# A two-layer decoder on one core: a shared first convolution, identity products for TensorE, an earlier signal of the residual sum, and first keys laid down later

## The reference, cut to what matters

```
layer 0: softmax attention, 16 heads of 16 features; queries and keys through a
         3-tap convolution; per token tau, delta = sigmoid(w2 . gelu(depthwise
         3-tap convolution of x)); scores * tau + delta; then output projection
         cross attention to the context (softmax over features)
         8 experts, each token to its best 2, 640 slots each, relu
layer 1: causal linear attention with rotary angles
         context-query attention (c2q, q2c), linear over 4 parts
         16 experts, each takes 64 tokens of an entry (after Sinkhorn), gelu
```

## Time and profile before

| | |
|---|---|
| median of 3 runs | 2402.48 us (2394.66 to 2403.40) |
| profiled execution, its own time | 2401.25 us |
| its span in the trace | 2399.5 us |
| PE busy | 2083.1 us, 87% |
| DVE, ACT, POOL busy | 1568.1, 1270.4, 1097.1 us |
| mean granted PE clock | 0.937 of full |

### The profile page before, as it was taken

The page is one execution under the profiler, slowest core; times in us unless marked ns, Lnnn a source line. Parts: engine busy times, 40 slices in busy tenths (PEclk is TensorE's granted clock), DMA queues, the critical chain, the costliest instruction groups (busy, mean ns, idle before and its releaser), DMA issues. The chain is left out here.

```text
span 2399.5 us, 47249 instructions
## 1 busy us (share of the span) xinstructions
PE 2083.1 (87%) x17382; PEld 1468.1 (61%) x17382; DVE 1568.1 (65%) x3061; ACT 1270.4 (53%) x2058; POOL 1097.1 (46%) x1252
## 2 busy tenths in 40 slices
PE   7599999995887299967999969961999999999998
PEld 5466666663665177755666648841667667676675
DVE  5378888885897655547888746667555555555553
ACT  2266666664343166635666635532664664654653
POOL 2988888861221122226655314301545445455443
PEclk9799999997998599989999969985999999999999
DMA  5000000000002233311111000041434434434332
GB/s 226 1 2 1 0 0 0 0 1 6 8 9 71 77 130 114 114 44 32 32 30 26 0 11 18 15 141 69 114 75 110 105 80 109 101 101 100 87 78 30
DMA packets 66919, 136.00 MB, mean 57 GB/s; under 512 B 11201, under 2 KB 52369, under 8 KB 59921
## 3 DMA queue, kind: packets, MB, share of 16 engines
q1 hardware_dynamic: 37264, 87.65, 10.5%
q0 software_dynamic: 29568, 47.21, 10.0%
HBM read 100.22 MB, written 34.60 MB: 56 GB/s over the span
## 5 line engine op out<-in xcount | busy, mean ns | idle before, releaser
L3375 ACT ACTIVATE f_h<-bank,f_b 128x512 f32<-128x512 f32 x256 | 176.1, 688 | 275.6 <-PE bank L176 268.9
L3418 DVE TENSOR_TENSOR f_hidlo<-f_h,f_hidhi 128x512 f16<-128x512 f32 x256 | 177.1, 692 | 165.7 <-ACT f_hidhi L3376 161.9
L176 PE MATMUL ring<-f_w2hi,f_hidhi 128*128 128x256 f16 x1024 | 279.2, 273 | 5.9 <-DVE f_hidlo L3418 3.6
L176 PE MATMUL ring<-f_w2lo,f_hidhi 128*128 128x256 f16 x1024 | 279.1, 273 | 0.0
L176 PE MATMUL ring<-f_w2hi,f_hidlo 128*128 128x256 f16 x1024 | 279.1, 273 | 0.0
L3475 POOL DMA_INDIRECT out<-f_y,f_to_row x128 | 203.4, 1589 | 96.6 <-DVE f_y L3433 50.7
L176 PE MATMUL bank<-f_xthi,f_w1hi 128*128 128x512 f16 x512 | 194.6, 380 | 0.0
L176 PE MATMUL bank<-f_xtlo,f_w1hi 128*128 128x512 f16 x512 | 194.6, 380 | 0.0
L176 PE MATMUL bank<-f_xthi,f_w1lo 128*128 128x512 f16 x512 | 194.5, 380 | 0.0
L3376 ACT ACTIVATE f_hidhi<-bank,f_b 128x512 f16<-128x512 f32 x256 | 174.3, 681 | 0.0
L3460 POOL DMA_INDIRECT f_xg<-tokens,f_from_row x128 | 149.2, 1166 | 47.9 <-issue 34.6
(11 more groups left out here) (621 smaller groups left out, 6012.8 us busy)
## 6 DMA issues: line engine op xcount, KB each, us to landing
f_raw<-in_e_w SPq DMA_DIRECT2D x32, 1024.0 KB
c_raw<-in_e_w SPq DMA_DIRECT2D x16, 1024.0 KB, 5.1
slots_out<-c_y SPq DMA_DIRECT2D x40, 128.0 KB, 4.1
x<-in_x SPq DMA_DIRECT2D x1, 4096.0 KB
tokens<-c_xn SPq DMA_DIRECT2D x16, 256.0 KB, 2.7
tokens<-f_xn SPq DMA_DIRECT2D x16, 256.0 KB, 2.5
out<-x SPq DMA_DIRECT2D x1, 4096.0 KB, 14.3
wb<-in_wb SPq DMA_DIRECT2D x1, 3096.0 KB, 33.0
```

What stands on the lines that cost most here:

```text
L176: mm = pe.matmul(out, left[a], right[b], start=first and n == 0, stop=last and n == 2)
L3375: act.activation(h32[n % 4][:, :], src, ACT.Gelu_apprx_tanh, bias=bias).then_inc(sig["h_full"], 1)
L3418: dve.tensor_tensor(hid_v[1][:, it, at], h32[n % 4][:, :], hid_v[0][:, it, at], ALU.subtract).then_inc(sig["h_lo"], 1)
```

## The change

It has four parts.

1. In the `front` of the first attention GpSimd makes only part 0 of the convolution of twins[0]; VectorE makes parts 1 to 3 (`convolve_first`): for each of the two groups of a part one scaled copy and two multiply-adds of 128x256, with a wait on its own counter after each tap. They stand behind both `low_x` and ahead of `take_q`. ACT's first `gelu` waits for the three parts too. GpSimd's order becomes: part 0 of twins[0], part 0 of twins[1], `high_keys` of twins[0], parts 1 to 3 of twins[1]. The turns after that are as before.
2. `keep_busy(pe, mem, bank, n)` issues n products of the fp16 identity with itself, 128 by 512 columns, into a bank that is free then. They stand at nine places: 16 in the front of the first attention; 8 and 16 in that of the cross attention; 28 at the start of the 8 experts; 22 and 32 in the front of the linear attention, the 22 behind a new wait for w_low_made; 12 ahead of the context attention and 6 in each of its first pair's six `products`; 18 and 12 in the first `turn_rows` of the 16 experts. That is 200 in all.
3. `residual_add` raises x_updated with the sum, waits for x_updated itself, and then makes the statistics. Its unused branch with a bias goes.
4. The later `high_keys` of part 1 (first keys laid down later).

```diff
+def keep_busy(pe, mem, bank, n):
+    for _ in range(n):
+        pe.matmul(bank.rearrange("p (r c) -> p r c", c=P), mem.ident16[:, :],
+                  mem.ident16[:, :].unsqueeze(1).to_broadcast([P, 4, P]), start=True, stop=True)
...
-def residual_add(dve, sig, mem, b, now, ready, update, bias, order, tmp):
+def residual_add(dve, mem, b, now, ready, update, updated):
     dve.wait_ge(ready, now)
     xb = mem.x[:, bass.ds(b * W2, W2)]
...
-        order.step(dve.tensor_tensor(xb, xb, update, ALU.add))
-    order.wait()
+    dve.tensor_tensor(xb, xb, update, ALU.add).then_inc(updated, 1)
+    dve.wait_ge(updated, now)
     for t in range(NT):
-        ins = dve.bn_stats(mem.stats[...], mem.x[...])
-    return ins
+        dve.bn_stats(mem.stats[...], mem.x[...])
...
 first attention, PE front
                     sum_tau_delta(w, j)
+                    keep_busy(pe, mem, twins[1].ring_bank[1], 16)
 ACT front
+                    act.wait_ge(sig["first_convolved"], 3)
                     gelu(w, j)
 POOL
-                    if part == 3:
+                    if part == (0 if first else 3):
                         pool.sem_inc(u["conv_done"], 1)
                 def front(w, j, v):
-                    for u in twins:
-                        for part in range(4):
-                            convolve(u, j, part)
-                        if u.p == 0:
+                    convolve(w, j, 0, first=True)
+                    for part in range(4):
+                        convolve(twins[1], j, part)
+                        if part == 0:
                             high_keys(w, j)
 DVE
+                def convolve_first(u, i, part):
+                    groups = (2 * part, 2 * part + 1)
+                    dve.wait_ge(u["x_pad_ready"], i.now)
+                    for k in range(TAPS):
+                        for c in groups:
+                            w = mem.cols[:, dwc + TAPS * c + k:dwc + TAPS * c + k + 1]
+                            x, out = u.xp[:, (c // 2) % 2, k:k + S], u.dw_v[:, c, :]
+                            if k == 0:
+                                ins = dve.tensor_scalar(out, x, w, mem.cols[...], ALU.mult, ALU.add)
+                            else:
+                                ins = dve.scalar_tensor_tensor(out=out, in0=x, scalar=w, in1=out, ...)
+                        order.step(ins)
+                        order.wait()
+                    dve.sem_inc(sig["first_convolved"], 1)
                 def front(w, j, v):
                     for u in twins:
                         low_x(u, j)
+                    for part in range(1, 4):
+                        convolve_first(w, j, part)
                     take_q(w, j)
 cross attention, PE front
+                    keep_busy(pe, mem, w.bank[2], 8)
                     turn_x(w, j)
+                    keep_busy(pe, mem, w.bank[2], 16)
 8 experts, PE
+                keep_busy(pe, mem, bank[5], 28)
                 turn_slots(Turn(0, 1), True)
 linear attention, PE front
+                    pe.wait_ge(sig["w_low_made"], 1)
+                    keep_busy(pe, mem, twins[1].high, 22)
                     turn_x(w, j)
...
                     project_v(w, j)
+                    keep_busy(pe, mem, twins[1].high, 32)
                     turn_queries(w, j, 0)
 context attention, PE
+                        if ago is None:
+                            keep_busy(pe, mem, twins[0].out, 6)
+                        else:
...
                 pe.wait_ge(sig["w_q_ready"], 1)
+                keep_busy(pe, mem, twins[0].out, 12)
 16 experts, PE, turn_rows
+                        if first and k == 2:
+                            keep_busy(pe, mem, bank[5], 12)
...
+                keep_busy(pe, mem, bank[5], 18)
                 turn_rows(Turn(0, 1), True)
```

More of the change, by code:

```diff
@@ L517, in transpose_entry @@
     return ins
-def residual_add(dve, sig, mem, b, now, ready, update, bias, order, tmp):
+def residual_add(dve, mem, b, now, ready, update, updated):
     dve.wait_ge(ready, now)
     xb = mem.x[:, bass.ds(b * W2, W2)]
-    if bias is not None:
-        order.step(dve.tensor_tensor(tmp, xb, update, ALU.add))
-        order.wait()
[L527 to L530, removed]
-        order.step(dve.tensor_tensor(xb, xb, update, ALU.add))
-    order.wait()
+    dve.tensor_tensor(xb, xb, update, ALU.add).then_inc(updated, 1)
+    dve.wait_ge(updated, now)
     for t in range(NT):
-        ins = dve.bn_stats(mem.stats[:, bass.ds((b * NT + t) * 6, 6)], mem.x[:, bass.ds(b * W2 + t * D, D)])
-    return ins
+        dve.bn_stats(mem.stats[:, bass.ds((b * NT + t) * 6, 6)], mem.x[:, bass.ds(b * W2 + t * D, D)])
 def transpose_stack(pe, mem, out, stack, t):
@@ L978, in _, with convolve @@
                 order = Order(pool, sig["pool_step"])
-                def convolve(u, i, part):
+                def convolve(u, i, part, first=False):
                     if part == 0:
@@ L1130, in update @@
                 def update(u, i):
-                    residual_add(dve, sig, mem, i.before * 2 + u.p, i.now, u["out_made"], u.high, None, order, None
-                                 ).then_inc(u["x_updated"], 1)
+                    residual_add(dve, mem, i.before * 2 + u.p, i.now, u["out_made"], u.high, u["x_updated"])
+                def convolve_first(u, i, part):
[6 more added lines that the diff above has]
+                            if k == 0:
+                                ins = dve.tensor_scalar(out, x, w, mem.cols[:, dwb + c:dwb + c + 1], ALU.mult, ALU.add)
+                            else:
+                                ins = dve.scalar_tensor_tensor(out=out, in0=x, scalar=w, in1=out, op0=ALU.mult,
+                                                               op1=ALU.add)
+                        order.step(ins)
+                        order.wait()
+                    dve.sem_inc(sig["first_convolved"], 1)
                 def front(w, j, v):
@@ L2809, in products @@
                     def products(n):
-                        if ago is not None:
+                        if ago is None:
+                            keep_busy(pe, mem, twins[0].out, 6)
+                        else:
                             for m in range(2 * n, 2 * n + 2):
@@ L2970, in update @@
                     dve.wait_ge(u["x_biased"], i.now)
-                    residual_add(dve, sig, mem, value(dve, i.before * 2 + u.p), i.now, u["out_made"], u.out, None,
-                                 order, None).then_inc(u["x_updated"], 1)
+                    residual_add(dve, mem, value(dve, i.before * 2 + u.p), i.now, u["out_made"], u.out, u["x_updated"])
                 def low_c2q(u, q, i):
```

## The result

| | before | after |
|---|---|---|
| median of 4 and 4 runs on one chip | 2402.94 us (2394.66 to 2405.68) | 2375.57 us (2374.43 to 2376.68) |
| profiled execution, its own time | 2401.25 us | 2375.18 us |
| its span | 2399.5 us | 2373.4 us |
| mean granted clock | 0.937 | 0.955 |

The ratio of the runs is 0.9887, with a 95% interval from 0.9872 to 0.9902: the kernel is 27.4 us faster by the medians, 26.1 us by the two profiled executions. The forecast was 2378, from 2367 to 2390.

What follows compares the result with a forecast made beforehand. Bounds: GpSimd's convolution in the first front, TensorE's half clock after waits, project_v's waits for statistics. Terms summed to -23.9 us from 2401.25, giving 2377.4, raised to 2378 towards the runs' median; range 2367 to 2390.

Steps and rivals of the forecast that it cites:

- The convolution, -11.0: First attention's front: sharing the convolution between GpSimd and VectorE saves 11.0 us; first gelu at 72.4 instead of 80.67.
- The second gelu, 96.3: First attention's front: GpSimd's second convolution ends 10.1 us earlier, so the second gelu starts at 96.3 instead of 106.36.
- The signal, -2: First attention, project_v's 14 waits for statistics: raising x_updated with the sum gains 0.15 us each time, 2 us in all.
- Cross attention, -1.5: Cross attention's front: 8 and 16 identity products bring 2.9 us of half-clock work down to 1.45, saving 1.5 us.
- 8 experts, -3.2: Start of the 8 experts: 28 identity products in a 9.5 us wait speed the half-clock work behind, saving 3.2 us.
- Linear attention, -2.5: Linear attention's front: 22 products give 1.6 us at the turn and first projection, 32 give 0.9; together 2.5 us.
- Context attention, -2: Ahead of and inside the context attention's first pair: 12 and 36 identity products raise the clock, saving 2 us net.
- 16 experts, -1.7: First turn_rows of the 16 experts: 12 products let transposes and first products run at full clock, saving 1.7 us.
- products useless: Rival for all fronts: the identity products bring nothing, leaving convolution dates and the earlier signal; 2389 us, chance 0.18.
- No collision: Rival in the first attention's front: VectorE and GpSimd don't hold each other up; 8 us more gained, 2370 us, chance 0.10.
- VectorE starves: Rival in the first attention's front: GpSimd gets two instructions in at each VectorE wait; gain only 7.5, 2381 us, chance 0.09.

Runs made afterwards that it cites:

- the kernel with 83 more: The changed kernel plus 83 more identity products in five further waits; 2371.93 us, ratio 0.9898 to the kernel before on its chip.
- the first two groups: Follow-up kernels ran in three groups of four, each on one chip beside the kernel before, whose median there was 2403.09, 2397.17 and 2417.72 us.

## Why the prediction was right, point by point

The forecast total was 2.4 us above the median after. The terms are less good than the sum, and that the sum came out is in part luck: the linear attention gave 4.3 us more than forecast, most of it in code that the change leaves alone, and that made up for the signal and the 16 experts, which gave nothing (2 and 1.7 us forecast), and for the context attention.

- **The convolution, -11.0: measured -12.5 and -12.1** in the two kernels without products. The first gelu's date came out (72.4 forecast, 72.38 measured), but not by its terms. VectorE's part alone takes 2.72 us and not 2.4, so three take 8.2 in place of 7.1; GpSimd held it up by 4.7 in place of 5.8. Two errors of one microsecond cancelled; what the trace bears out is that the two engines hold each other up. The Trainium skill, page "SBUF — State Buffer", section "SBUF: two separate sides", says of the port pair that VectorE and GpSimd share that one of them holds it for the whole instruction, and this trace has its mark: multiply-adds of 0.48 us that last up to 1.49 beside GpSimd, and 0.485 in the median without it.
- **The second gelu, 96.3: measured 93.64.** This step failed. I charged GpSimd all of VectorE's 7.1 us. By the rows it would have ended part 0 of twins[1] alone at 57.04 + 2 x 5.73 = 68.5, and it ended it at 70.7 (69.43 and 1.26): 2.2 us of delay. Its sums (1.26 to 1.33 us) were hardly held up, only its copies (0.55 to 1.14). Against that I had the keys wait for nothing, and GpSimd, being early, waited 3.18 us for them. Of the wait ahead of `tau_delta` not 3 us but nothing is left.
- **The signal, -2: measured 0** (ratio 1.0000, interval 0.1% to each side; section -0.35). I named the reason, VectorE's full list, and gave it 0.15 us an entry all the same. TensorE waits for the queries' copy (7.0 us) where it waited for statistics (8.9).
- **Cross attention, -1.5: measured -2.8**, -3.6 with the products alone, but also -1.6 in one trace without any; with such differences between traces the term can't be told from 1.5.
- **8 experts, -3.2: measured -3.9 and -4.1**, and -0.2 to -0.8 in the three kernels without products. It rests on a margin of one microsecond in a transfer's arrival, as the kernel with 83 more showed.
- **Linear attention, -2.5: measured -6.8 and -5.7.** The mis-sized term. Its front gave 2.0 us, 1.3 of them by the time at which the stacked queries are there; behind the 32 products the clock did not hold (3.4 us of work at the half level, against 4.0 before). The other 4.8 us lie at its end, in code that the change leaves alone: of 1388 to 1411 before, 14.9 us of work ran at the half level, after only 2.6. The windows of before and of after:

```profile
1388.00:1408.00 20.00, 15.47 (x113) 8.83 (x110) 4.01 (x8) 3.24 (x6) 0.00 (x0) 0.51 0.00 0
```
```profile
1368.00:1383.00 15.00, 9.90 (x94) 5.87 (x93) 3.65 (x7) 2.99 (x5) 0.00 (x0) 0.89 0.00 0
```

The traces without products, the repeat of before among them, have 5.5 to 9.6 us there, and sections of -1.7 to -3.8; so about 2 us of it were bad luck of the one trace that I worked from. Why the five with products in the first two groups had 2.7 us at most, while those of the third had 2.4, 2.7, 12.4 and 14.9, stays open.
- **Context attention, -2: measured -0.5**, but the good case of before was the one profiled. Against the four other traces without products (+3.9, +3.9, +3.8, -0.2, so +2.8 in the mean) it gives 3.4.
- **16 experts, -1.7:** measured +0.1 in the full change, -1.5 with the products alone. The 12 products gave 1.5 us against the section's start in both. The 18 gave nothing: they ended 4.3 us before the first rows came, and those transposes took 1.97 us as before. In the full change the last expert took the gain back. Ahead of its second layer TensorE waits 2.13 us, in the traces of before too; in this trace the clock fell behind that wait and 3.4 us of work ran at the half level, with the products alone and in the first trace of before it did not fall:

```profile
2341.33 0.27 PE L176 MATMUL ring<-f_w2hi,f_hidhi 128*128 128x256 f16 x1 [2.13 <-issue]
```
```profile
2341.80:2345.20 3.40, 3.40 (x19) 2.42 (x17) 0.00 (x0) 0.00 (x0) 0.00 (x0) 0.50 0.00 0
```

This fall comes in five of the nine traces with products and in none of the five without; whether the products bring it stays open.

The rival "products useless" (2389) is refuted by their 12.7 us, and 2391 is what the kernel without them took. "No collision" (first gelu 66.6) and "VectorE starves" (78) are refuted by 72.38. At every one of the places the clock was at the full level by the last product. It fell again 1.2 us into the work behind the 32 of the linear attention, and it was down when the first rows came behind the 18 of the 16 experts.

## What to carry over

A gain in a front is read from what ends last behind it: an engine freed of 17 us of work was worth 12.5, an earlier signal to an engine that another one paces was worth nothing. Products that keep TensorE's clock up pay where dense work of TensorE is what ends last behind them; size them to the latest arrival (a gap of 1.1 us behind them kept the clock here, one of 2.2 us lost it and 3.7 us with it), not to the one traced. Profile the kernel before more than once when single terms are 2 us: here two traces of one program differed by about 2 to 4 us in three sections.

## What the runs showed of the hardware that I had not expected

- VectorE and GpSimd slow each other unequally: VectorE's 8.2 us of convolution became 12.9, GpSimd's 11.5 us beside it became 13.7.
- In one trace of before TensorE worked 25.3 of the 35 us from 1411 to 1446 and the clock was granted at the half level until 1445; in the other, with the same matmuls, it rose at 1423.
- In the four traces of one chip three to five of ACT's 13 to 16 waits for TensorE in the linear attention's loop lasted about 4.2 us, where the ten traces of the other chips show 2.55 to 2.72 us each time; its input was ready for about 1.5 us of it. The kernel before took 14.6 us more there than on the chip of the first group, the changed kernel 7.9 us more than at first.
